# Attention, first block: the step-size product as one pass over stacked high and low parts of 16 rows, state inputs copied apart

## What is computed

```python
x = x + xattn0(layernorm(x), ctx, Wq, bq, Wk, bk)     # softmax attention
x = x + ffn0(layernorm(x), gate_cp, up_cp, down_cp)   # weights from spline control points
x = x + mamba(ctx, layernorm(x), in_proj, conv, x_proj, dt_proj, ...)
x = x + moe(layernorm(x), ...)                        # top 8 of 32 experts
```

```python
x = einsum('bld,ed->bel', ctx, in_proj_w)
x = silu(causal_conv(x, conv_w) + conv_b)             # u in the kernel
x_dbl = einsum('bdl,ed->bel', x, x_proj_w)            # 48 rows
dt_low, Bm, Cm = split(x_dbl, [16, 32], axis=1)       # 16 rows each
dt = softplus(einsum('brl,dr->bdl', dt_low, dt_proj_w) + dt_proj_b)
```

## Time and profile before

| | us |
|---|---|
| median of 3 runs | 1583.55 |
| lowest and highest | 1582.53 and 1583.83 |
| the profiled execution, device time | 1581.82 |
| its span, first to last instruction | 1580.0 |
| granted clock of TensorE, mean over the span | 0.957 |

### The profile page before, as it was taken

One profiled execution on the slowest core, in us unless ns is written; L12 is line 12 of the kernel. 1 busy time (PEld: TensorE's weight loads), 2 busy tenths in 40 slices (PEclk: granted clock), 3 DMA queues, 4 the chain that ended last, 5 costly groups with the idle time before them and its releaser, 6 DMA issues. The chain is left out here.

```text
span 1580.0 us, 26519 instructions
## 1 busy us (share of the span) xinstructions
PE 1450.5 (92%) x6469; PEld 1080.0 (68%) x6470; DVE 1152.2 (73%) x2064; ACT 916.8 (58%) x1415; POOL 1056.9 (67%) x654
## 2 busy tenths in 40 slices
PE   7999878999999999999975559999999989898997
PEld 3444456666666666666644338878888979787896
DVE  5777898888888888888878786656566656565654
ACT  5776687666666666766646664444444544444442
POOL 2222187999999999999941235666666666666675
PEclk8999989999999999999997759999999999999999
DMA  8232356899889888989879416889898888888876
GB/s 304 83 121 97 126 159 133 173 184 233 179 195 206 196 192 193 221 184 197 178 144 346 154 36 162 189 193 196 195 202 191 188 203 187 193 183 203 194 145 121
DMA packets 106336, 283.62 MB, mean 180 GB/s; under 512 B 16641, under 2 KB 18978, under 8 KB 95010
## 3 DMA queue, kind: packets, MB, share of 16 engines
q0 software_dynamic: 43520, 155.57, 49.4%
q1 hardware_dynamic: 60242, 122.80, 26.1%
q10 hardware_dynamic: 2512, 4.52, 0.8%
HBM read 151.95 MB, written 135.08 MB: 182 GB/s over the span
## 5 line engine op out<-in xcount | busy, mean ns | idle before, releaser
L1141 POOL TENSOR_TENSOR B_E<-B_dtu,B_BC 128x512 f32<-128x512 f32 (+3 forms) x121 | 309.6, 2664 | 16.7 <-DMA B_BC<-bc_d 16.4
L2065 POOL DMA_INDIRECT out_x<-D_y,D_rows x144 | 241.6, 1677 | 78.8 <-issue 42.0
L874 ACT ACTIVATE bank<-B_dtv,negA 128x512 f32<-128x512 f32 x256 | 173.1, 688 | 156.5 <-DVE B_E L1009 95.5
L1009 DVE TENSOR_TENSOR_SCAN B_E<-bank,B_E 128x512 f32<-128x512 f32 x192 | 229.7, 1211 | 42.4 <-ACT bank L874 39.2
L1147 POOL TENSOR_TENSOR B_E<-B_E,B_BC 128x1536 f32<-128x1536 f32 x64 | 234.1, 3659 | 31.6 <-DVE B_E L1009 26.1
L2030 POOL DMA_INDIRECT D_rows<-rows_d,D_source x144 | 150.8, 1047 | 136.7 <-DMA out_x<-D_y,D_rows 71.8
L791 PE MATMUL bank<-B_Wd,B_inter 128*128 128x512 f32 x512 | 229.4, 601 | 10.0 <-DVE X L996 6.2
L1891 ACT ACTIVATE D_xT_hi<-bank 128x512 fp32r<-128x512 f32 x147 | 87.7, 596 | 229.5 <-PE bank L1800 229.4
L1811 PE MATMUL bank<-W_gu_hi,D_xT_hi 128*128 x584 | 202.9, 347 | 18.7 <-ACT D_xT_hi L1891 18.5
L1953 DVE TENSOR_TENSOR D_xT_lo<-bank,D_xT_hi 128x512 fp32r<-128x512 f32 x147 | 101.2, 688 | 137.3 <-ACT D_xT_hi L1891 132.9
L1812 PE MATMUL bank<-W_gu_lo,D_xT_hi 128*128 x584 | 199.6, 342 | 0.0
(11 more groups left out here) (323 smaller groups left out, 3271.5 us busy)
## 6 DMA issues: line engine op xcount, KB each, us to landing
y_d<-B_E POOLq DMA_DIRECT2D x64, 1024.0 KB, 10.6
B_BC<-bc_d SPq DMA_DIRECT2D x128, 256.0 KB, 6.2
W_raw_gu<-in_wgu SPq DMA_DIRECT2D x64, 384.0 KB
W_raw_d<-in_wd SPq DMA_DIRECT2D x64, 256.0 KB
X<-in_x SPq DMA_DIRECT2D x4, 1024.0 KB, 9.0
y_d<-A_du SPq DMA_DIRECT2D x4, 1024.0 KB, 4.0
dt_d<-A_dtv SPq DMA_DIRECT2D x4, 1024.0 KB, 3.9
dtu_d<-A_dtu SPq DMA_DIRECT2D x4, 1024.0 KB, 4.0
```

The lines of the kernel that those rows point to most:

```text
L874: act.activation(dA[m % 2][:, :], dtv[:, c, :], ACT.Exp, scale=negA[:, c, n:n + 1]).then_inc(dA_done, 1)
L1009: v.tensor_tensor_scan(state, dA[m % 2][:, :], E[:, s % NR, c, :], 0.0, ALU.mult, ALU.add).then_inc(s_done, 1)
L1141: g.tensor_tensor(E[:, s % NR, c:end, :], dtu[:, at:at + end - c, :], spread(BC[op % NBC][:, :], end - c), ALU.mult).then_inc(dbu_done, 1)
L2065: g.indirect_dma_start(a["out"], bass.IndirectOffsetOnAxis(ap=rows[i][:, ROW - 1:ROW].bitcast(U32), axis=0), ysb[:, i, :], None, compute_o ...
```

## The change

The 16 rows of `dt_low` are computed three times, by a stationary operand `xpT` that holds the 16 columns of the weight at 0, 32 and 64 and is now 128 columns wide. So bank 6 has three copies of `dt_low`, at rows 0, 32 and 64, zeros between them, and `Bm`, `Cm` at rows 96 to 127. ACT copies rows 0 to 95 to `xdbl`, now an fp32r tile, and DVE overwrites rows 64 to 79 with the low part. `dpT` is 96 rows high in the same way, with high, low and high part of `dt_proj_w`. One fp32r matmul over the 96 rows then gives high*high + high*low + low*high. `dpT` is made in batch 0 from a raw copy, which is loaded into a part of `pos`, by one ACT copy and one DVE subtraction. `Bm` and `Cm` are copied by a second ACT instruction to a tile of their own, `xbc`, from which `bc_d` is stored. The wait for `stored` stands before that second copy. To make room, the raw spline powers are loaded into a part of `dtu`, and ACT's copy of them is moved from the end of batch 0 to before the softplus.

```diff
-        xpT = sb("xpT", [P, KC, R + 2 * NS])
-        dpT, dpb, Dp = sb("dpT", [R, DI]), sb("dpb", [P, KC]), sb("Dp", [P, KC])
+        xpT = sb("xpT", [P, KC, XP])
+        dpT, dpb, Dp = sb("dpT", [XD, DI], F32R), sb("dpb", [P, KC]), sb("Dp", [P, KC])
...
-        xdbl = sb("xdbl", [R + 2 * NS, L])
+        xdbl, xbc = sb("xdbl", [XD, L], F32R), sb("xbc", [XP, L])
...
-                    mm = pe.matmul(bank[6][0:R + 2 * NS, :], xpT[:, k, :], u[:, k, :], start=k == 0, stop=k == KC - 1)
+                    mm = pe.matmul(bank[6][0:XP, :], xpT[:, k, :], u[:, k, :], start=k == 0, stop=k == KC - 1)
                 mm.then_inc(xd_ps, 1)
                 pe.wait_ge(xT_sb, b * 4 + 4)
-                pe.wait_ge(xd_sb, b + 1)
+                pe.wait_ge(xd_lo, b + 1)
                 for k in range(KC):
-                    pe.matmul(bank[O_BANK[k]][:, :], dpT[:, k * P:(k + 1) * P], xdbl[0:R, :], start=True, stop=True).then_inc(dt_ps, 1)
+                    if O_BANK[k] == 6:
+                        pe.wait_ge(xd_sb, b + 1)
+                    pe.matmul(bank[O_BANK[k]][:, :], dpT[:, k * P:(k + 1) * P], xdbl[0:XD, :], start=True, stop=True).then_inc(dt_ps, 1)
...
                     act.activation(alog[:, :, :], alog[:, :, :], ACT.Exp).then_inc(negA_exp, 1)
+                    act.activation(dpT[:, :], raw_dp, ACT.Copy).then_inc(negA_exp, 1)
...
                 act.wait_ge(xd_ps, b + 1)
+                act.activation(xdbl[0:XD, :], bank[6][0:XD, :], ACT.Copy).then_inc(xd_hi, 1)
+                act.wait_ge(xd_lo, b + 1)
                 if b:
                     act.wait_ge(stored, b * 64)
-                act.activation(xdbl[:, :], bank[6][0:R + 2 * NS, :], ACT.Copy).then_inc(xd_sb, 1)
+                act.activation(xbc[XD:XP, :], bank[6][XD:XP, :], ACT.Copy).then_inc(xd_sb, 1)
...
                     act.activation(attT[:, k, :], bank[2 + k][:, :], ACT.Copy).then_inc(aT_act, 1)
+                if b == 0:
+                    act.wait_ge(ld_r, 16 * 15)
+                    act.activation(powers[:, :, :, :], raw_pw[:, :, :, :], ACT.Copy)
...
-                if b == 0:
-                    act.wait_ge(ld_r, 16 * 15)
-                    act.activation(powers[:, :, :, :], raw_pw[:, :, :, :], ACT.Copy)
...
+                if b == 0:
+                    v.wait_ge(negA_exp, 2)
+                    v.tensor_tensor(dpT[32:32 + R, :], raw_dp[32:32 + R, :], dpT[32:32 + R, :], ALU.subtract).then_inc(negA_exp, 1)
+                    v.wait_ge(negA_exp, 3)
                 for m in range(4):
                     v.tensor_scalar(att[:, m, :], att[:, m, :], rinv[:, m:m + 1], None, ALU.mult).then_inc(att_done, 1)
+                    if m == 0:
+                        v.wait_ge(xd_hi, b + 1)
+                        v.tensor_tensor(xdbl[64:64 + R, :], bank[6][64:64 + R, :], xdbl[64:64 + R, :], ALU.subtract).then_inc(xd_lo, 1)
```

More of the change, by code:

```diff
@@ L36 @@
 EPS = 1e-5
+XD = 3 * 32
+XP = XD + 2 * NS
 NCTRL = max(16, int(INTER * D / 128.9))
@@ L177, in block_a @@
         taps, table, select = sb("taps", [P, 3, INTER]), sb("table", [P, INTER]), sb("select", [P, NSEL])
-        raw_pw, coef = sb("raw_pw", [NSEL, KC, 2, P]), sb("coef", [NSEL, 3, L], F32R)
+        coef = sb("coef", [NSEL, 3, L], F32R)
+        raw_dp, raw_pw = pos[0:XD, 0, :], dtu[0:NSEL, :, :].rearrange("p k l -> p (k l)")[:, 0:KC * 2 * P].rearrange("p (k h n) -> p k h n", k=KC, h=2)
         LOW = slice(2 * NSEL // 3, NSEL)
@@ L188, in block_a @@
         aT_ps, aT_act, aT_dve, o_ps, x1_done = (sem(n) for n in ("aT_ps", "aT_act", "aT_dve", "o_ps", "x1_done"))
-        xd_ps, xd_sb, dt_ps, dt_abs, dt_pos = (sem(n) for n in ("xd_ps", "xd_sb", "dt_ps", "dt_abs", "dt_pos"))
+        xd_ps, xd_hi, xd_lo, xd_sb, dt_ps, dt_abs, dt_pos = (sem(n) for n in ("xd_ps", "xd_hi", "xd_lo", "xd_sb", "dt_ps", "dt_abs", "dt_pos"))
         sp_exp, sp_one, sp_ln, sp_fix, dt_done = (sem(n) for n in ("sp_exp", "sp_one", "sp_ln", "sp_fix", "dt_done"))
@@ L209, in _ @@
                 sp.dma_start(dst, a[name]).then_inc(ld_qk, 16)
-            for dst, name in ((xpT[:, :, :], "xpT"), (dpT[:, :], "dpT"), (dpb[:, :], "dpb"), (Dp[:, :], "Dp"), (alog[:, :, :], "alog")):
+            for dst, name in ((xpT[:, :, :], "xpT"), (raw_dp, "dpT"), (dpb[:, :], "dpb"), (Dp[:, :], "Dp"), (alog[:, :, :], "alog")):
                 sp.dma_start(dst, a[name]).then_inc(ld_w, 16)
@@ L218, in _ @@
                     load_ctx(b + 1)
-                for wait, dst, src in ((xd_sb, bc_d[b], xdbl[R:R + 2 * NS, :]),
+                for wait, dst, src in ((xd_sb, bc_d[b], xbc[XD:XP, :]),
                                        (du_done, y0_d[b], du[:, :, :]),
@@ L2080, in chunked, with spread @@
         return w.reshape(-1, P, w.shape[-1]).transpose(1, 0, 2)
+    def spread(w):
+        out = np.zeros(w.shape[:-1] + (XD,), np.float32)
+        for n in range(0, XD, 32):
+            out[..., n:n + R] = w
+        return out
     def windows(cp):
@@ L2098 @@
         "convb": x["L1_xattn_conv_b"].reshape(KC, P).T,
-        "xpT": chunked(x["L1_xattn_x_proj_w"].T), "dpT": x["L1_xattn_dt_proj_w"].T,
+        "xpT": chunked(np.concatenate([spread(x["L1_xattn_x_proj_w"].T[:, :R]), x["L1_xattn_x_proj_w"].T[:, R:]], 1)),
+        "dpT": spread(x["L1_xattn_dt_proj_w"]).T,
         "dpb": x["L1_xattn_dt_proj_b"].reshape(KC, P).T, "Dp": x["L1_xattn_D"].reshape(KC, P).T,
```

## The result

The changed kernel took 1568.45 us as the median of four runs (1562.19 to 1569.08), beside 1583.69 for the kernel before on the same chip: a ratio of 0.990, with a 95% interval of 0.986 to 0.994. The profiled execution took 1569.08, with a span of 1567.3 us, 12.7 less than before.

What follows compares the result with a forecast made beforehand. PE was taken to bound block A; savings of 2.3, 3.95, 3.3 and 0.3 us in batches 1, 2, 0 and 3 summed to 9.85, so 1583.55 would become 1573.7 us, range 1572.0 to 1578.8.

Steps and rivals of the forecast that it cites:

- What bounds block A: Block A: PE, busy 42.73 of batch 1's 43.5 us, sets each batch's end; sparing PE between input products shortens it.
- The new path behind C: Each batch, from ACT's copy of bank 6: absolute values from C+1.97, output product at C+5.5, next input product at C+21.8.
- C: Start of ACT's copy of bank 6 in each batch, just after PE's x_dbl product; C+5.5 means 5.5 us later.
- The batches: Block A's forecast savings: batch 1 2.3 us, batch 2 3.95, batch 0 3.3, batch 3 0.3; sum 9.85.
- A term that I had at nothing: x_dbl product with 128 columns: taken to cost nothing, as 96 and 128 columns both run at 0.43 an entry.
- the first rival: Clock still falls behind C in each batch: 1.3 us a batch lost in batches 0 to 2, 1577.6 us; chance 0.30.
- The clock falling in each batch all the same: Behind C: transposes at half clock end at C+6.4, output product starts there; gain 5.95 us, time 1577.6; chance 0.30.
- The clock staying low through the output product: Half clock through output and coefficient products, all 16.3 us: slower than before, 52 us over three batches; chance 0.04.
- the gain not being handed on: Block B, the experts or `c_lo` set the end instead: up to all 9.85 us lost, 1580 to 1583.5; chance 0.05.
- That the product would be no shorter: Step-size product behind C: fp32r no shorter than before, 2.3 us less gain, 1576 us; chance 0.05.
- The rule on transposes: Skill's claim that full clock "doesn't engage" for transposes; C to C+5.5 would hold almost nothing that counts; not taken as forecast.

Runs made afterwards that it cites:

- the high part on 16 rows: Changed kernel with low parts left out of the step-size product (one fp32r pass over 16 high rows) and without DVE's subtraction in each batch: 1564.7 us, four runs.

## Why the prediction was wrong

The direction and the mechanism were right, the size was too small, and the range too narrow.

**What bounds block A: right.** PE is busy for 38.67 us of 40.60, the length of batch 1, and the next input product follows the output product without a wait for `c_lo`. The profile of after shows it from 56.6 to 97.2:

```profile
56.60:97.20 40.60, 38.67 (x115) 18.66 (x114) 33.99 (x53) 31.34 (x46) 8.86 (x5) 1.00 0.29 111
```

**The new path behind C: right up to the absolute values, then mis-sized.** High copy 0.59, subtraction 0.69, product at C+1.46, absolute values from C+1.97: each within 0.02. The step that failed is the pace behind that. I counted four absolute values as four times 0.69, which ends at C+4.8, and DVE's four positive parts as 3.32, both from the earlier trace rows. The 3.32 had been measured while each quarter of the product came 0.86 after the one before: that pace was PE's, not DVE's. The 0.69 is the length of one instruction and is the same after the change (0.68 to 0.70), but in a row each starts some 0.57 after the one before, which has not ended by then. With all quarters ready, four absolute values take 2.42, and four positive parts 2.73. So ACT's first copy of the transposed attention came 0.5 earlier, at C+4.27, and the output product with it, C+5.02 instead of C+5.5. PE's wait of 0.38 there ends with ACT's copy, so it is ACT's term that set the size. The stretch from there to the next input product was 16.39, where I had 16.3. Next was C+21.41 instead of C+21.8.

**The batches.** Batch 1: 2.72 where I had 2.3. Batch 2: 4.34 where I had 3.95. Batch 0: I had charged 0.65 for the subtraction of `dpT` ahead of the scalings; it was hidden here, since C itself came later: DVE was ready for the low part 0.36 before the high copy had come, and next was at C+21.41 as everywhere. With the high part on 16 rows, where C of batch 0 is 32.57, it was not hidden: PE waited 0.50 for the scalings. C of batch 0 was 33.52 and not 32.28 because the clock was at its half from 24.25 to 27.5 in this execution and from 21.3 to 24.7 before, which is no part of the change (in seven other profiles of kernels with the wide product it stands between 32.57 and 33.39). So 3.11 where I had 3.3. Batch 3: 1.05 where I had 0.3; here the same term runs through the softplus. ACT's exponential starts 0.78 earlier behind C, DVE's part of the softplus, which waits 0.21 for ACT, 0.83 earlier, and the store of `dtu` 0.80 earlier; the other 0.25 lie between that store and the end of the block, and their cause is open.

**A term that I had at nothing.** From the input product to the next C it takes 19.24 instead of 19.37, in all eight profiles of kernels with the wide x_dbl product, 0.13 less for each of three batches. Some 0.09 of it lie between the start of the energies and the start of the x_dbl product (3.44 instead of 3.53). I had looked for a cost there only. No run changes the width alone.

The terms together: 9.85 forecast, 11.6 measured in block A. By that alone the time would have been 1572.1 (1583.69 less 11.6), just inside the range. But the median moved by 15.2 in the first four runs and 13.1 in six others, so it was the part beyond block A, 1.5 to 3.6 us, that put the time outside. It belongs to no term of the sum. About 2 us of the 3.6 is scatter: the kernel before had 1583.7 in four runs and 1582.6 in 25, the changed one 1568.45 in four runs and 1569.3 in six. Whether the remaining one or two are scatter too is open. What I left out is this scatter: I took the spread of three runs (1.3 us) for that of the kernel, and 25 runs of the kernel before spread over 21 us. It goes with the granted clock: of those 25, the seven with a mean clock over the span of 0.953 or less took 1588.5 us on average, the seven with 0.957 or more (up to 0.960) 1579.2. In which block the clock differed is not on record for these runs. A range that ends 1.7 us below the forecast can't hold for a median of four such runs.

**The rivals.** The clock falling in each batch all the same: no, in 0 of 8 batches of the two profiles of after. The gaps were as foreseen (1.50 ahead of the product, 0.38 ahead of the output), and they did not matter; in the kernel with the short product on 16 rows the clock did fall in one batch. The clock staying low through the output product, the gain not being handed on: no. That the product would be no shorter: no, four entries in 1.16.

**The rule on transposes.** The transposes ran at full clock behind C, 16 in 1.97 us, in every profile of after. By the rule of the Trainium skill (TensorE: Matmul & The Clock Gate, "Part 4: PE-mode transpose"), the full clock would not have been engaged for them, and the first rival would have come true. The measurement decides against it, for the f32 transposes of this kernel. The kernel with 96 rows in f32 shows it more sharply, in batch 0: the clock was at its half from 22.15 to 25.55, PE ran nothing but the 16 transposes of the tokens in that time, and then the clock rose. Timeline of PE, then PE by stretch:

```profile
22.10 3.65 PE L268 MATMUL bank<-ident,A_xn 128*128 128x128 f32 x16 [2.48 <-ACT A_xn L325]
```

```profile
22.25:25.50 3.25, 3.25 (x16) 0.50 0.44 120
25.50:28.00 2.50, 2.50 (x8) 0.99 1.01 416
```

**What my reading of before missed.** I called batch 1 "at full clock" up to its output product, and read a path of C+6.91 from it. But its transposes took 2.78 where 16 take 1.91 at full clock, so even that path held 0.9 of half clock. The kernel with 96 rows in f32 shows the true one, C+6.0, and how the gain is made up. Block A's end goes from 193.68 (16 rows) to 183.14 with 96 rows, and to 180.55 by the single pass with its low parts. Counted from C of batch 0, which varies from execution to execution for the reason given above, block A takes 160.29, 150.48 and 147.03: 9.8 us by the rows alone, and 3.45 by the single pass. So about three quarters of what the change brings in block A would have come with zeros in the weights, with no high and low part at all.

## What to carry to other kernels

- Where the granted clock falls beside a matmul with few rows, try filling rows before shortening anything: here the same product over 96 rows, 80 of them with zero weights, took the same 3.67 us, the clock no longer fell behind it, and block A ended 10.5 us earlier, 9.8 of them behind the first C.
- The time of a run of instructions, read where the engine waits for each piece of its input, is the pace of whoever feeds it; and the length of one instruction times their number is too much where the next one starts before it has ended. For a case in which all pieces are ready, take the term from a stretch where the engine runs back to back.
- Take the scatter of a kernel from many runs, or leave room for it: three runs within 1.3 us said nothing about a spread of 21.

## What was not expected of the hardware

- TensorE went to 1.2 GHz, during or just behind a f32 product over 16 rows (3.67 us at full clock) with a gap of 0.77 or 0.78 ahead of it, in 12 of 12 batches, and in none of 24 where 96 rows were at work, with gaps of 0.78 (long product) and of 0.73 to 1.50 (short). Of four batches with a product of 1.17 us over 16 rows and a gap of 0.77 it fell in one, the one with a second gap of 0.50. In the two f32 kernels that differ in the rows alone, the engine was equally busy in time.
- An absolute value of 128x512 from PSUM on ACT takes 0.69 us, and four in a row take 2.42, since each starts some 0.57 after the one before; four of DVE's positive parts take 2.73 in a row and 3.32 with a wait ahead of each.
- The stretch that holds the x_dbl product took 19.24 us in every kernel where its weights have 128 columns and 19.37 where they have 48. The wider product cost nothing, and the stretch was 0.13 shorter.
- The clock rose from its half behind a stretch in which PE ran nothing but f32 transposes (22.15 to 25.55 in the kernel with 96 rows in f32).
